# Attention probabilities turned by VectorE through an HBM scratch instead of TensorE transposes, with scores computed four steps ahead, in a one-core attention and FFN kernel

## The reference

```python
x = x + xattn(layernorm(x), ctx, Wq, Wk, Wv, Wo)     # x, ctx: (8, 128, 512) float32
x = x + ffn(layernorm(x), weight, bias, gate_w, in_channel_scale, out_channel_scale)
# xattn: keys and values from concat([ctx, layernorm(x)]), so 256 keys per batch
#   q: 32 heads of 128; k, v: 4 groups of 128 (8 query heads share a group)
#   attn = softmax(q k^T / sqrt(128)); out = (attn v) @ Wo
# ffn: routing = softmax(xf @ gate_w.T); 8 experts
#   out = (xf * (routing @ in_channel_scale)) @ sign(weight).T * (routing @ out_channel_scale) + bias
```

## Time and profile before

| | |
|---|---|
| median of 3 runs | 738.95 us (738.42 to 739.14) |
| span of the profiled execution, first to last instruction | 737.0 us; no time of its own is recorded beside the span |
| PE busy | 725.1 us (98%), 3880 matmuls |
| DVE busy | 400.4 us (54%) |
| ACT busy | 363.7 us (49%) |
| POOL busy | 266.6 us (36%) |
| DMA | 60.59 MB, 82 GB/s on average |
| granted TensorE clock | full speed over the whole span (mean 1.000) |

### The profile page before, as it was taken

The page is one execution under the profiler, slowest core; times in us unless marked ns, Lnnn a source line. Parts: engine busy times, 40 slices in busy tenths (PEclk is TensorE's granted clock), DMA queues, the critical chain, the costliest instruction groups (busy, mean ns, idle before and its releaser), DMA issues.

```text
span 737.0 us, 11712 instructions
## 1 busy us (share of the span) xinstructions
PE 725.1 (98%) x3880; PEld 617.3 (84%) x3880; DVE 400.4 (54%) x742; ACT 363.7 (49%) x945; POOL 266.6 (36%) x316
## 2 busy tenths in 40 slices
PE   7999999999999999999999999999999999999996
PEld 5888888888888888888888888888888888888874
DVE  4552233664366436643664366436643664768876
ACT  3343324663466346634663466346634663465642
POOL 4243003441344134413441344134413441445554
PEclk9999999999999999999999999999999999999999
DMA  9566459110112320101223201012242010000001
GB/s 322 206 228 235 172 214 314 42 55 5 58 59 86 95 104 0 57 0 57 63 79 103 96 0 57 0 57 72 74 124 74 1 58 1 1 0 16 15 30 58
DMA packets 28418, 60.59 MB, mean 82 GB/s; under 512 B 2088, under 2 KB 2088, under 8 KB 27360
## 3 DMA queue, kind: packets, MB, share of 16 engines
q1 hardware_dynamic: 28384, 60.15, 24.0%
HBM read 41.27 MB, written 18.87 MB: 82 GB/s over the span
## 4 chain that ended last, share of the span: by engine, by line
PE 95%; DVE 2%; issue 1%; POOL 1%; DMA 1%; ACT 0%; SPq 0%; DVEq 0%; ACTq 0%; POOLq 0%
PE bank L947 48%; PE bank L1076 23%; PE bank L1059 12%; PE bank L1042 7%; PE bank L1158 1%; PE bank L1113 1%; DMA raw_a<-in_L_xattn_Wv 1%; PE bank L956 1%; DVE wq_pair L647 0%; PE bank L964 0%; PE bank L1105 0%; DVE stats L650 0%; PE bank L1128 0%; DVE acc L743 0%; PE bank L1091 0%
## 5 line engine op out<-in xcount | busy, mean ns | idle before, releaser
L351 POOL TENSOR_TENSOR prob<-prob,rsum 128x512 f32<-128x512 f32 x128 | 133.6, 1046 | 218.0 <-DVE rsum L731 218.0
L1076 PE MATMUL bank<-wo_pair,oT 128*128 128x512 f32 x768 | 203.5, 403 | 0.0
L947 PE MATMUL bank<-xT,wq_pair 128*128 128x512 f32 x768 | 184.0, 392 | 0.0
L947 PEld LDWEIGHTS bank<-xT,wq_pair 128*128 128x128 f32 x768 | 142.0, 188 | 28.8
L1076 PEld LDWEIGHTS bank<-wo_pair,oT 128*128 128x128 f32 x768 | 136.9, 188 | 24.8
L496 ACT ACTIVATE prob<-bank,nmax 128x256 f32<-128x256 f32 x256 | 118.6, 470 | 24.8 <-DVE nmax L725 24.8
L947 PEld LDWEIGHTS bank<-kg,qT 128*128 128x128 f32 x768 | 108.0, 189 | 9.5
L947 PE MATMUL bank<-kg,qT 128*128 128x256 f32 x768 | 112.7, 282 | 0.0
L313 POOL TENSOR_TENSOR wo_pair<-raw_b,wo_pair 128x512 fp32r<-128x512 f32 x32 | 41.0, 1312 | 189.2 <-ACT wo_pair L417 189.2
L417 ACT ACTIVATE pT<-bank 128x512 fp32r<-128x512 f32 x128 | 75.5, 597 | 59.2 <-PE bank L1042 59.2
L718 DVE SCALAR_TENSOR_TENSOR qT<-bank,qT 128x512 fp32r<-128x512 f32 x64 | 44.2, 691 | 107.8 <-ACT qT L487 107.8
(11 more groups left out here) (85 smaller groups left out, 576.7 us busy)
## 6 DMA issues: line engine op xcount, KB each, us to landing
v_park<-v_stage SPq DMA_DIRECT2D x8, 1024.0 KB, 4.3
raw_a<-in_L_xattn_Wq SPq DMA_DIRECT2D x8, 1024.0 KB, 6.8
raw_b<-in_L_xattn_Wo SPq DMA_DIRECT2D x8, 1024.0 KB, 5.4
k_park<-k_stage SPq DMA_DIRECT2D x8, 1024.0 KB, 3.9
kg<-k_park SPq DMA_DIRECT2D x32, 256.0 KB, 3.0
vg<-v_park SPq DMA_DIRECT2D x32, 256.0 KB, 3.2
craw<-in_ctx SPq DMA_DIRECT2D x8, 256.0 KB, 5.8
acc<-in_x SPq DMA_DIRECT2D x8, 256.0 KB, 5.9
```

The source lines that it names most:

```text
L351: nc.gpsimd.tensor_tensor(prob[:, p], prob[:, p], rsum[:, p].unsqueeze(2).to_broadcast([P, 2, KEYS]), ALU.mult).then_inc(prob_ready[p], 1)
L947: last = nc.tensor.matmul(dst, left(a, c), right(b, c), start=(n == 0), stop=(n == 3 * chunks - 1))
L1076: last = nc.tensor.matmul(wo_bank[:, :], oT[:, s, h, :], wo_pair[:, w, h, :], start=((s, w) == TERMS[0] and h == 0), stop=((s, w) == TERMS ...
```

## The change

Per pair and step, `transposes`, `pt_half` and `pt_rest` are replaced by:

- `turn` (DVE): one 32x32 block transpose of prob[p] (128x512, SBUF to SBUF) into p_turned.
- `park_p` and `fetch_p` (SP): one DMA of 512 KB per step writes p_turned to a scratch p_park in HBM, and four DMAs of 128 KB read it back into p_low so that each 32-row block lies on its own partitions. Keys come in the order (block, chunk), so K is staged in that order too.
- `p_half` (ACT, one copy of 128x1024 into p_high) and `p_rest` (POOL, one subtraction of 128x1024 in place in p_low), per step for all four heads.

The order is new on every engine. At step t: attend t, scores of t+4 (pair 0), one q_unit of the next quad, scores of t+4 (pair 1), project_out of t (the same step, all four heads). Pair 0 of a batch is normalised and turned in the step of its scores, pair 1 one step later. Wo is split at step 0 of a quad (heads 0 and 2 on DVE, 1 and 3 on POOL), Wq at steps 5 to 7 and 1. SP's loop is written out. In the last quad the FFN pieces hang on this order. yT and oscale now share space with kg.

On SP:

```diff
+            def park_p(g, qd, t):
+                for p in range(2):
+                    sp.wait_ge(turned[p], steps(g, qd, t + 1))
+                sp.dma_start(p_park[t % 4], p_turned[:, t % 2].rearrange("p k h q -> p (k h q)")
+                             ).then_inc(p_parked[t % 2], 16)
+            def fetch_p(g, qd, t, first=False):
+                sp.wait_ge(p_parked[t % 2], 16 * pairs(g, qd, t))
+                if not first:
+                    sp.wait_ge(av_ready, steps(g, qd, t - 1))
+                rows = p_park[t % 4].rearrange("(i r) e -> r i e", r=32)
+                for j in range(QB):
+                    sp.dma_start(
+                        words(p_low[32 * j:32 * (j + 1), t % 2]).rearrange("r i c q -> r i (c q)"),
+                        rows[:, :, j * KC * QH * 32:(j + 1) * KC * QH * 32]).then_inc(p_in[t % 2], 16)
...
+            def step(g, qd, t, last):
+                final = last and qd == QUADS - 1
+                if not (final and t + 2 >= B):
+                    fetch_p(*step_after(g, qd, t, 2))
+                if not (final and t + LEAD - 1 >= B):
+                    park_p(*step_after(g, qd, t, LEAD - 1))
```

On POOL a step is:

```diff
+            def step(g, qd, t, last):
+                final = last and qd == QUADS - 1
+                if not (final and t + LEAD - 1 >= B):
+                    normalise(*step_after(g, qd, t, LEAD - 1), 1)
+                if t == 0:
+                    wo_rest(g, qd, 1)
+                if not (final and t + 1 >= B):
+                    p_rest(*step_after(g, qd, t, 1))
+                if t == 0:
+                    wo_rest(g, qd, 3)
+                if t >= B - 3 and not last:
+                    wq_rest(*quad_after(g, qd, 2), t - (B - 3))
+                if t == 1 and not final:
+                    wq_rest(*quad_after(g, qd, 1), 3)
+                if final and t >= 1:
+                    make_rstd(B + t - 1)
+                if final and t >= 2:
                     bias_add(t - 2)
+                if not (final and t + LEAD >= B):
+                    normalise(*step_after(g, qd, t, LEAD), 0)
+                if final and t >= 3:
+                    ffn_add(t - 3)
```

On ACT:

```diff
+            def step(g, qd, t, last):
+                if not (final and t + 1 >= B):
+                    p_half(*step_after(g, qd, t, 1))
                 if t == 0:
+                    wo_half(g, qd, 0)
+                    wo_half(g, qd, 1)
                 o_half(g, qd, t)
+                if t == 0:
+                    wo_half(g, qd, 2)
+                    wo_half(g, qd, 3)
+                if final and b >= 1:
                     z_half(b - 1)
+                if ahead:
+                    exps(*ahead, 0)
```

ACT ahead of the loop, and then POOL ahead of it:

```diff
+            for t in range(LEAD):
+                exps(0, 0, t, 0)
+                if t < LEAD - 1:
+                    exps(0, 0, t, 1)
+                q_half(0, 0, QH + t, first=True)
+            for h in range(3):
+                wq_half(0, 1, h)
+            exps(0, 0, LEAD - 1, 1)
+            p_half(0, 0, 0)
```

```diff
+            for h in range(3):
+                wq_rest(0, 1, h)
+            normalise(0, 0, LEAD - 1, 0)
+            p_rest(0, 0, 0)
```

On PE:

```diff
+            def step(g, qd, t, last):
+                final, b = last and qd == QUADS - 1, t - 2
+                ahead = None if final and t + LEAD >= B else step_after(g, qd, t, LEAD)
                 attend(g, qd, t)
...
+                if ahead:
+                    scores(*ahead, 0)
+                if not final:
+                    q_unit(*quad_after(g, qd, 1), t)
+                if final and b >= 1:
                     ffn_product(b - 1, (HI,))
+                if final and b >= 0:
                     y_transpose(b)
+                if final and b >= 1:
                     ffn_product(b - 1, (LO,))
+                if ahead:
+                    scores(*ahead, 1)
+                if final and b >= 0:
+                    logits(b)
+                project_out(g, qd, t, (0, 1))
...
+                if final and b >= 0:
                     route_transpose(b)
+                project_out(g, qd, t, (2, 3))
+                if final and b >= 0:
                     channel_scales(b)
```

More of the change, by code:

```diff
@@ new lines, in _ @@
+            for b in range(LEAD):
+                load_kv(0, b)
+            for t in range(LEAD - 1):
+                park_p(0, 0, t)
+                if t < 2:
+                    fetch_p(0, 0, t, first=True)
+                load_kv(0, LEAD + t)
+            load_kv(0, B - 1)
+            def step(g, qd, t, last):
[5 more added lines that the diff above has]
+                if t == 1 and not final:
+                    sp.wait_ge(wo_lo, count(g, 2, qd, 2))
+                    sp.wait_ge(wo_lo_pool, count(g, 2, qd, 2))
+                    load_wo(*quad_after(g, qd, 1))
+                if t == 3 and not final:
+                    ng, nqd = quad_after(g, qd, 1)
+                    sp.wait_ge(wq_lo, count(ng, QH, nqd, QH))
+                    if last:
+                        sp.dma_start(raw_a[:, :, :], ffn_w.rearrange("(c p) n -> p c n", p=P)
+                                     ).then_inc(ffn_in, 16)
+                    else:
+                        load_wq(*quad_after(g, qd, 2))
+                if qd == QUADS - 1 and not last:
+                    for p in range(2):
+                        sp.wait_ge(s_ready[p], steps(g, qd, t + 1))
+                    sp.wait_ge(av_ready, steps(g, qd, t + 1))
+                    load_kv(g + 1, t)
@@ L277, in group @@
-                    load_wo(g, qd + 1)
-                if not last:
-                    qd = QUADS - 1
-                    for b in range(B):
-                        for p in range(2):
-                            sp.wait_ge(s_ready[p], steps(g, qd, b + 1))
-                        sp.wait_ge(av_ready, steps(g, qd, b + 1))
-                        load_kv(g + 1, b)
-            with sp.Fori(0, G - 1) as g:
-                group(g, False)
-            group(G - 1, True)
+                    for t in range(B):
+                        step(g, qd, t, last)
@@ L290, in _ @@
+            for g in range(G):
+                group(g, g == G - 1)
             for b in range(B):
@@ new lines, in step @@
+                if t >= B - 3 and not last:
+                    wq_half(*quad_after(g, qd, 2), t - (B - 3))
+                if t == 1 and not final:
+                    wq_half(*quad_after(g, qd, 1), 3)
+                if not final:
+                    q_half(*quad_after(g, qd, 1), t)
+                if final and t == 1:
+                    for c in range(HC):
+                        sgn_copy(c)
+                if final and b >= 0:
+                    yt_copy(b)
+                if ahead:
+                    exps(*ahead, 1)
```

545 lines of the change are left out of this document (209 added, 336 removed).

## The result

| kernel | median | runs | ratio to before (95% interval) |
|---|---|---|---|
| before | 738.68 us | 737.92 to 739.14, 4 runs | |
| as changed | 749.45 us | 743.00 to 752.68, 4 runs | 1.0137 (1.0092 to 1.0183) |

The change makes the kernel 10.8 us **slower**. The forecast was 731 us, faster, with 749.45 just outside the range. Two things are to be explained: the profiled execution, the fastest of the four (743.0 us, span 741.2), ran 12 us over the forecast, and the others took 6 to 10 us more still, of a kernel whose predecessor repeats within 1.3 us (four runs here, and within 2.5 us over all 30 runs of it beside this and the later kernels, 737.9 to 740.4).

The account below looks back on a forecast made before the run. PE, busy 98% of the span, was taken as the bound. Terms -56.3 + 5.6 + 7.9 + 30.7 + 4.3 = -7.8; span 737.0 - 7.8 + 1.95 (median above span) = 731 us, chance 0.50, range 708 to 748.

Parts of the forecast that it names:

- the last quad: No q_unit fills its steps; late z pieces, the lock with p_rest and a late gate stretch it to 93.9 us: +30.7.
- the tail: From the channel_scales of batch 5 to the end: 22.2 us, with 12.5 idle on PE against 8.2 before: +4.3.
- transposes off PE: 16 pieces per quad, 128 in all, at 0.44 us leave PE: -56.3 us; a common step needs 8.31.
- do the others fit: Common step: DVE at 4.9 us (a turn's cost T taken as 0.69), ACT near 4.8, POOL 5.6, against PE's 8.31.
- do the chains fit: Common step: chains between engines, with HBM landings of at most 3.9 us, end in time, so there is no wait.
- first step of a quad: wo_rest behind p_rest and the lock comes late for project_out: +0.8 us for each of 7 quads, 5.6 us.
- ahead of the loop, +7.9: Before attend 0: p_half and p_rest stand behind weight copies and splits, so attend 0 ends 7.9 us later.
- R1: The last quad covers itself: two thirds of its 30.7 us are not lost; 711 us, chance 0.25.
- R2: Turns take the DVE-POOL lock too and wait for p_rest, costing in first steps and last quad: +10, 741 us, chance 0.12.
- R3: Common step: the turn makes DVE the bound, kernel slower from 2.5 us per turn, about 770 at 2.7; chance 0.08.
- R4: Common step: the HBM fetch lands in 6.8 us and p_half is late, +1.2 in 56 steps; near 798 us, chance 0.05.
- wrong in kind if PE's matmuls themselves became slower: Sign named beforehand that the forecast fails in kind: slower PE matmuls, or waits in common steps; no size given.

Follow-up runs that it names:

- fillers: The changed kernel with 127 spare matmuls put in front of PE's waits ahead of the loop, in the last quad and in the tail: 733.73 us.
- again: The changed kernel run once more, unedited, with a second profiled execution: 751.08 us, that execution's span 749.6 us.
- experiment 4: The changed kernel with only the last quad's order on DVE and ACT edited, pieces PE waits for put first: 722.28 us, ratio 0.9777.
- experiment 6: The changed kernel with both of POOL's weight splits before p_rest in the first step of a quad: 744.48 us, ratio 1.0072.
- experiment 7: The changed kernel with each turned block written to HBM twice, turn's completion waiting for both writes: 751.33 us, ratio 1.0145.

## Why the prediction was wrong

*Failed: the last quad and the tail, and with them the sum.* Both terms were hand schedules at full-clock prices, taken from a kernel whose clock never fell. "Adding up step by step in this way I get ... 93.9" used 1.4 us for half of project_out; behind a wait it took 2.91. No term stood for what a wait does to the matmuls after it: it was put at nothing without a reason. The runs put the missing term at 17.4 us (751.1 against 733.7 with fillers), by profiled spans 9.1 to 17.5. In the profiled execution, 12.2 us over the forecast's 729.05 span, it splits by segment into 2.3 ahead of attend 8, 0.1 in the loop, 2.7 in the last quad and 7.0 behind the last attend; with fillers these are 1.8, 0.1, 1.0 and 0.1. In "again", whose time is nearer to most runs, they are 3.2, 0.3, 10.1 and 7.0.

*The tail, +4.3,* was 22.2 us from the last channel_scales of the loop; it took 29.3. Here the last ffn_product's eight matmuls are at 3.75 us, where the filled kernel has 2.12, and the logits of batch 6 at 1.88 instead of 1.06. Filled, the whole segment is within 0.1 us of the forecast.

*The last quad, +30.7:* the steps were forecast as 9.1, 8.3, 15.3, 14.5, 12.8, 11.8, 11.8, 10.3. In the profiled execution they are 9.0, 8.3, 15.7, 14.3, 15.4, 11.8, 11.8, 10.2. All but one are right to 0.4 us. Their three causes stand in the trace: z_rest or ffn_norm beside p_rest, z_half behind z_make, gate_max behind the turn (in steps 2 and 3). The fifth is 2.6 over. But that execution was the fastest, and its agreement is in part luck. In "again" steps 3 to 6 are 17.1, 16.4, 14.3 and 12.8, with equal waits for y and z_half. One reading of a row was off: a y pass beside a POOL operation does not wait for its end "and then run" its full 0.55 us, it ends 0.3 us behind it (0.29 in the row, 0.28 in experiment 4's).

*Right: transposes off PE.* The step is 8.28 (8.31). That the six quads agree to 0.1 us (403.8, forecast 403.7) is luck: 48 steps of 0.03 less make 1.4, and the first steps of the quads lose 1.4 more than was forecast. *Right: do the others fit, do the chains fit.* No wait stands in a common step, T is 0.70 (0.69), p_rest 2.40 (2.5), the landings 3.1 and 3.0 (at most 3.9). *Too small: first step of a quad.* 0.8 for each was forecast, 4.8 for these six; it is 0.5 in four and 2.1 and 2.2 in the two behind the branch, 6.2 in all. There ACT stands 2.3 us under "issue" (it waits for nothing that the profile shows) ahead of p_half, which the forecast did not have. The mechanism that it named, wo_rest behind p_rest, is confirmed by experiment 6, which takes 4.7 of these 6.2 us away.

*Nearly right: ahead of the loop, +7.9.* The two waits, 4.22 and 2.99, were forecast to the place and within 0.8 us in sum. The segment is 2.3 us over for two other reasons: PE comes to the first wait 1.9 us late (136.1 against 134.1; it waits 0.7 for a qT and 0.6 for prob before), and the attend, scores and q_unit behind the waits take 2.0 us more at the low clock (the q_unit 3.54 instead of 2.91). Against that stand 0.7 less wait and the 0.8 of a first step, which the first quad does not lose.

*The rivals.* R1 (711, the last quad covers itself) did not happen as written, but its premise was sound: the waits are a matter of order, and experiment 4 takes 60% of those for y and z_half away (23.8 to 9.6 us). R2 and R3 fall with the turn's 0.70 us, R4 with the landings of 3.0 us and experiment 7. None of the four was the one that came. The range stopped at 748, and beyond it stood only R3 and R4; a rival "PE's clock falls behind waits" was missing on that side. The line "wrong in kind if PE's matmuls themselves became slower" is what happened.

The Trainium skill has the rule that was left out ("TensorE: Matmul & The Clock Gate", Part 1: The HAM clock gate): PE's clock has two levels and is set by how busy PE has lately been. The trace agrees: 0.50 behind the waits, in 142 to 147 and from 640 to 646 us, and 1.00 in the loop. The rule would have spoken against opening waits here. The length of one wait alone does not settle the level, though: here the same 1.2 us was followed by either.

## What to carry to other kernels

When a change takes work off a TensorE that is 98% busy and opens waits on it, price every matmul behind each wait at both clock levels, not only the wait: some 31 us of waits (15.2, 8.6, 4.2 and 3.0) cost 9 to 17 us more here. If a wait can't be reordered away, put spare matmuls in front of it, but no more than it has room for: 30 of them ahead of the loop took 7.0 us where the wait was 4.2, and gave back 1.4 us in all. And reorder first, since the order of the last quad alone gave 28.8 us and the fillers alone 17.4. When the runs of a kernel spread (743 to 753) while those of its predecessor do not (738 to 740), read the granted clock of the profiled executions before anything else.

## What was not expected of the hardware

- One program, with almost equal waits, ran its last quad in 86.3 us or in 93.7, by which steps were granted which clock. A single profiled execution, here the fastest of four, does not show it.
- A block transpose of 128x512 float32 on DVE takes 0.70 us and does not wait for a POOL operation that runs beside it, where a pass of one input of the same size (ffn_norm, 0.54 alone) takes 1.92.
- Four transposes in a row on PE cost 0.46 us, but a single one in their place 0.14 to 0.32: half of what such a group costs is that it is there.
